# Layer 0 of a two-layer model: the rows for the expert sort are scaled on VectorE instead of GpSimd, and the step order of layer 0 is made anew

## What is computed

```python
xn = _layernorm(x, axis=-1)
x = x + _L0_attn_ref(xn, ...) + _L0_ffn_ref(xn, ...)

def _L0_ffn_ref(x, gate_w, w1, w2, w3):      # 4096 tokens, 8 experts, 2 of them for each token
    scores = jax.nn.softmax(xf @ gate_w, axis=-1)
    top_scores, top_idx = jax.lax.top_k(scores, TOP_K)
    scale = jnp.zeros((T, E)).at[jnp.arange(T)[:, None], top_idx].set(top_scores)
    xs = scale.T[:, :, None] * xf[None, :, :]
    h = jax.nn.silu(jnp.einsum('etd,edh->eth', xs, w1)) * jnp.einsum('etd,edh->eth', xs, w3)
    y = jnp.einsum('eth,ehd->etd', h, w2)
    out = y.sum(axis=0)
```

## Time and profile before

| | us |
|---|---|
| median of 3 runs | 1774.85 (1771.12 to 1778.79) |
| the profiled execution, its own time | 1774.8 |
| its span, first to last instruction | 1773.1 |
| of it layer 0 (last DVE instruction ends at 551.1; layer 1's first at 557.4) | 551 |
| PE busy | 1620.7 |
| DVE busy | 1477.5 |
| POOL busy | 1367.5 |
| ACT busy | 1349.2 |

### The profile page before, as it was taken

How to read it: one execution, slowest core, us unless ns; L and a number is a source line. 1 busy time by engine, 2 the same in 40 slices (tenths; PEclk the granted TensorE clock), 3 DMA queues, 4 the chain that set the end, 5 groups by cost and what they waited for, 6 DMA issues and landing times.

```text
span 1773.1 us, 43498 instructions
## 1 busy us (share of the span) xinstructions
PE 1620.7 (91%) x13450; PEld 987.0 (56%) x13450; DVE 1477.5 (83%) x2750; ACT 1349.2 (76%) x3230; POOL 1367.5 (77%) x1114
## 2 busy tenths in 40 slices
PE   6788999999885888799999999999999999999988
PEld 3455687677563453465465456456556455545545
DVE  5787854356786989899989999999999999998996
ACT  5377877576663868878978978887887897797774
POOL 2059548862671188998999899899899999899995
PEclk9799999999988899999999999999999999999999
DMA  9633446596565743274373464445535446445430
GB/s 326 187 99 121 129 136 205 149 215 193 130 133 161 195 135 115 90 179 109 117 189 101 140 170 123 123 139 126 165 104 146 117 130 177 105 126 161 108 96 25
DMA packets 169963, 252.31 MB, mean 142 GB/s; under 512 B 31144, under 2 KB 114280, under 8 KB 169736
## 3 DMA queue, kind: packets, MB, share of 16 engines
q1 hardware_dynamic: 157448, 232.74, 46.5%
q0 software_dynamic: 12288, 16.79, 4.6%
HBM read 170.44 MB, written 75.86 MB: 139 GB/s over the span
## 4 chain that ended last, share of the span: by engine, by line
PE 37%; DVE 10%; issue 8%; ACT 7%; POOL 5%; DMA 1%; SPq 0%; DVEq 0%; ACTq 0%; POOLq 0%
PE bank L2382 32%; POOL HB L2333 3%; PE bank L2482 3%; DVE bank L2905 3%; DVE HB L2905 2%; ACT bank L2695 2%; POOL HB L2339 2%; DVE SU L2877 2%; ACT PR L2733 1%; DVE HB L2910 1%; ACT PT L2617 1%; PE bank L2510 1%; PE bank L2392 1%; DVE nmax L2936 0%; ACT PR L2726 0%
## 5 line engine op out<-in xcount | busy, mean ns | idle before, releaser
L2333 POOL TENSOR_TENSOR HB<-DD,BC 128x512 f32<-128x512 f32 x512 | 640.9, 1280 | 102.5 <-DMA DD<-SU 48.5
L2695 ACT ACTIVATE bank<-DD,A 128x512 f32<-128x512 f32 x512 | 349.4, 694 | 113.7 <-DVE HB L2910 72.4
L2339 POOL TENSOR_TENSOR HB<-HB,BC 128x512 f32<-128x512 f32 x256 | 324.4, 1284 | 30.7 <-DVE HB L2905 30.1
L2905 DVE TENSOR_TENSOR_SCAN bank<-bank,HB 128x512 f32<-128x512 f32 x256 | 310.8, 1214 | 21.9 <-ACT bank L2695 18.6
L2905 DVE TENSOR_TENSOR_SCAN HB<-bank,HB 128x512 f32<-128x512 f32 x256 | 310.0, 1211 | 10.3 <-ACT bank L2695 7.3
L2910 DVE TENSOR_TENSOR HB<-bank,BC 128x512 f32<-128x512 f32 x256 | 175.4, 685 | 15.9 <-DVE bank L2905 0.9
L2382 PE MATMUL bank<-HB,fold 128*32 128x512 f32 x1024 | 138.3, 612 | 20.5 <-DVE HB L2910 10.8
L743 POOL DMA_INDIRECT X<-expert_out_scratch,slot x64 | 108.0, 1687 | 40.6 <-issue 15.7
L2482 PEld LDWEIGHTS bank<-ident,PR 128*128 128x128 f32 x768 | 86.9, 142 | 82.9 <-issue 45.0
L2482 PE MATMUL bank<-ident,PR 128*128 128x128 f32 x768 | 114.6, 281 | 18.2 <-ACT PR L2733 8.7
L718 POOL TENSOR_SCALAR XSC<-XR,mv,scaled 128x256 f32<-128x256 f32 x64 | 94.2, 1476 | 41.1 <-DVE scaled L1383 36.4
(11 more groups left out here) (287 smaller groups left out, 3568.1 us busy)
## 6 DMA issues: line engine op xcount, KB each, us to landing
DD<-dd_scratch SPq DMA_DIRECT2D x488, 128.0 KB, 3.2
ROW<-row_scratch SPq DMA_DIRECT2D x64, 256.0 KB
BC<-ssm_scratch SPq DMA_DIRECT2D x128, 128.0 KB, 4.0
US<-us_scratch SPq DMA_DIRECT2D x32, 512.0 KB, 4.8
dd_scratch<-SU SPq DMA_DIRECT2D x16, 1024.0 KB, 6.0
us_scratch<-SU SPq DMA_DIRECT2D x15, 1024.0 KB, 6.5
XL<-sorted_scratch SPq DMA_DIRECT2D x78, 128.0 KB
expert_out_scratch<-YS SPq DMA_DIRECT2D x78, 128.0 KB
```

The costliest lines, as they stand in the source:

```text
L2333: done(pool.tensor_tensor(HB[:, c % HR], du, bc, ALU.mult), "dbu")
L2339: done(pool.tensor_tensor(h, h, bc, ALU.mult), "cg")
L2695: done(act.activation(PD[n % 2][:], delta, ACT.Exp, scale=A[:, k:k + 1]), "dA")
L2905: done(dve.tensor_tensor_scan(h if n % 2 else dA, dA, h, 0.0, ALU.mult, ALU.add), "scan")
```

## The change

The function `scaled_rows` and its branch move from POOL's block to DVE's; the instruction, its operands and its three waits stay the same. POOL keeps `sca`. The table `L0_ORDER` is made anew: all 2924 steps stand in it once, as before, with other positions. Against the old table a step of PE stands on average 4 places away within PE's own sequence, one of ACT and one of SP the same. DVE has 870 steps instead of 806, POOL 168 instead of 232. The positions of the steps next to the change are shown; of `tt`, the first tile's transposes, the first entries are 879 and 876 instead of 907 and 895 in the first group, and 1674 and 1679 instead of 1669 and 1672 in the second. Nothing of layer 1 changes.

```diff
-    "agg": [8, 55, 177, 223, 301, 476, 714, 901],
-    "rs1": [11, 57, 179, 225, 306, 649, 843, 905],
-    "xn1": [16, 14, 15, 17, 83, 74, 70, 79, 184, 187, 188, 185, 227, 228, 232, 230, 317, 359, 369, 370, 661, 656,
-        658, 655, 851, 854, 850, 853, 921, 920, 918, 923],
-    "xr": [34, 28, 30, 409, 417, 483, 473, 523, 527, 571, 598, 651, 674, 721, 745, 757, 794, 833, 856, 1096, 1089,
-        1181, 1163, 1240, 1274, 1357, 1345, 1403, 1433, 1481, 1505, 1565],
-    "sx": [357, 396, 406, 364, 415, 471, 463, 429, 499, 518, 522, 506, 550, 558, 586, 541, 641, 615, 663, 606, 713,
-        654, 739, 688, 752, 719, 782, 743, 824, 792, 848, 820, 1071, 1088, 1079, 1061, 1172, 1162, 1138, 1147, 1226,
-        1214, 1261, 1239, 1296, 1343, 1337, 1327, 1353, 1391, 1421, 1417, 1437, 1475, 1489, 1499, 1520, 1557, 1541,
-        1582, 1563, 1618, 1603, 1622],
-    "sca": [373, 441, 424, 386, 455, 490, 481, 448, 509, 526, 533, 514, 596, 580, 630, 569, 681, 626, 696, 617, 725,
-        672, 754, 704, 769, 732, 803, 761, 837, 812, 855, 831, 1132, 1116, 1094, 1108, 1189, 1180, 1220, 1204, 1247,
-        1301, 1286, 1271, 1317, 1361, 1380, 1371, 1400, 1430, 1447, 1460, 1480, 1527, 1504, 1547, 1534, 1587, 1576,
-        1593, 1614, 1638, 1630, 1646],
...
+    "agg": [11, 72, 186, 222, 287, 469, 744, 848],
+    "rs1": [14, 77, 188, 224, 292, 473, 749, 851],
+    "xn1": [20, 18, 19, 17, 81, 83, 87, 84, 192, 196, 195, 193, 230, 229, 231, 228, 351, 300, 355, 312, 529, 523,
+        534, 532, 761, 763, 758, 760, 877, 897, 889, 870],
+    "xr": [26, 2, 8, 393, 443, 453, 479, 522, 524, 557, 580, 645, 651, 704, 732, 770, 759, 818, 842, 1081, 1086,
+        1121, 1181, 1172, 1244, 1246, 1279, 1305, 1332, 1342, 1420, 1395],
+    "sx": [376, 389, 378, 438, 428, 449, 436, 475, 482, 516, 518, 507, 527, 553, 576, 548, 642, 592, 647, 586, 701,
+        660, 726, 725, 765, 694, 757, 753, 814, 747, 838, 824, 1067, 1074, 1078, 1069, 1100, 1115, 1176, 1136, 1154,
+        1167, 1235, 1178, 1212, 1239, 1275, 1242, 1267, 1300, 1320, 1326, 1322, 1335, 1365, 1413, 1392, 1386, 1432,
+        1457, 1448, 1453, 1462, 1510],
+    "sca": [380, 403, 390, 448, 432, 457, 441, 481, 487, 521, 538, 510, 531, 562, 579, 552, 644, 601, 657, 589, 708,
+        668, 737, 728, 773, 699, 762, 784, 817, 755, 841, 830, 1070, 1087, 1102, 1094, 1114, 1126, 1198, 1142, 1160,
+        1174, 1241, 1188, 1220, 1254, 1284, 1259, 1272, 1304, 1324, 1362, 1341, 1351, 1370, 1419, 1398, 1390, 1436,
+        1478, 1451, 1464, 1473, 1514],
...
@@ -706,18 +706,6 @@
                     after(pool, "agg", b, 0)
                     done(pool.tensor_tensor(columns(rstd1[:], b), ve1[:], half[:, 0:NT], ALU.pow), "rs1")
 
-                def scaled_rows(g, i):
-                    x, c = divmod(i, 2)
-                    b, t = batch_tile(g, x)
-                    after(pool, "n", g, RANKS - 1)
-                    k = TT * g + x
-                    pool.wait_ge(over[f"rows_in{k % XRS}"], 16 * (k // XRS + 1))
-                    n = 2 * TT * g + i
-                    if n >= SXS:
-                        pool.wait_ge(moved[f"sort_in{n % SXS}"], 16 * (n // SXS))
-                    done(pool.tensor_scalar(XSC[:, n % SXS], XR[:, k % XRS], columns(mv1[:, :, 0], b)[:, t:t + 1],
-                                            scaled[:, x, c:c + 1], ALU.subtract, ALU.mult), "sx")
-
                 def sort_rows(g, i):
                     x, c = divmod(i, 2)
                     after(pool, "sx", g, i)
@@ -753,8 +741,6 @@
                 for what, b, i in plan:
                     if what == "rs1":
                         input_rstd(b)
-                    elif what == "sx":
-                        scaled_rows(b, i)
                     elif what == "sca":
                         sort_rows(b, i)
                     elif what == "gad":
@@ -1383,6 +1369,18 @@
                         q = dve.tensor_tensor(scaled[:], weight[:], bc(rates, 2), ALU.mult)
                     done(q, "n")
 
+                def scaled_rows(g, i):
+                    x, c = divmod(i, 2)
+                    b, t = batch_tile(g, x)
+                    after(dve, "n", g, RANKS - 1)
+                    k = TT * g + x
+                    dve.wait_ge(over[f"rows_in{k % XRS}"], 16 * (k // XRS + 1))
+                    n = 2 * TT * g + i
+                    if n >= SXS:
+                        dve.wait_ge(moved[f"sort_in{n % SXS}"], 16 * (n // SXS))
+                    done(dve.tensor_scalar(XSC[:, n % SXS], XR[:, k % XRS], columns(mv1[:, :, 0], b)[:, t:t + 1],
+                                           scaled[:, x, c:c + 1], ALU.subtract, ALU.mult), "sx")
+
                 def factors(b):
                     after(dve, "rf", b, 0)
                     after(dve, "sq", b - 1, *range(NT))
@@ -1547,6 +1545,8 @@
                         decayed_values(b, i)
                     elif what == "dc":
                         decays(b, i)
+                    elif what == "sx":
+                        scaled_rows(b, i)
                     elif what == "at":
                         decayed(b, i)
                     elif what == "kv":
```

More of the change, by code:

```diff
@@ L87 @@
 L0_ORDER = {
-    "x_ld": [0, 19, 89, 191, 235, 376, 667, 859],
[4 rows of a table removed]
-    "agg": [8, 55, 177, 223, 301, 476, 714, 901],
[4 rows of a table removed]
-    "xtv": [23, 95, 197, 239, 384, 789, 869, 943],
-    "xta": [24, 97, 198, 242, 387, 783, 885, 940],
[6 rows of a table removed]
-    "vgc": [60, 38, 64, 33, 158, 171, 192, 203, 421, 513, 524, 508, 629, 734, 715, 758, 846, 862, 866, 877, 1650,
[4 rows of a table removed]
-    "smc": [44, 117, 206, 248, 634, 815, 910, 973],
[16 rows of a table removed]
-    "src": [96, 176, 368, 664, 796, 954, 1092, 1748],
-    "qt": [99, 118, 269, 261, 339, 307, 423, 389, 559, 546, 577, 592, 777, 785, 983, 959, 1196, 1120, 1272, 1402,
-        1696, 1667, 2392, 2032, 2448, 2409, 2476, 2502, 2656, 2731, 2720, 2771],
@@ L131 @@
-    "rst": [100, 178, 372, 670, 801, 960, 1254, 1750],
[5 rows of a table removed]
[L137 to L142, removed]
@@ L143 @@
-    "qsc": [123, 128, 214, 266, 351, 326, 501, 457, 549, 547, 660, 722, 930, 903, 1161, 1105, 1292, 1322, 1727, 1692,
[15 rows of a table removed]
-    "rld": [168, 174, 208, 215, 247, 273, 303, 350, 461, 434, 560, 512, 694, 699, 727, 748, 919, 887, 1222, 1145,
[35 rows of a table removed]
-    "ogt": [340, 365, 431, 395, 632, 618, 764, 770, 1003, 1007, 1062, 1076, 1896, 1835, 1968, 1857, 2322, 2362, 2460,
[6 rows of a table removed]
-    "sca": [373, 441, 424, 386, 455, 490, 481, 448, 509, 526, 533, 514, 596, 580, 630, 569, 681, 626, 696, 617, 725,
-        672, 754, 704, 769, 732, 803, 761, 837, 812, 855, 831, 1132, 1116, 1094, 1108, 1189, 1180, 1220, 1204, 1247,
-        1301, 1286, 1271, 1317, 1361, 1380, 1371, 1400, 1430, 1447, 1460, 1480, 1527, 1504, 1547, 1534, 1587, 1576,
-        1593, 1614, 1638, 1630, 1646],
@@ L206 @@
-    "ogc": [391, 410, 437, 425, 636, 627, 873, 776, 1012, 1015, 1068, 1085, 1903, 1839, 1987, 1869, 2327, 2369, 2467,
[55 rows of a table removed]
-    "yst": [955, 967, 1025, 1020, 1027, 1043, 1107, 1101, 1104, 1111, 1187, 1175, 1184, 1202, 1265, 1268, 1257, 1293,
[4 rows of a table removed]
-    "gad": [1716, 1689, 1647, 1656, 1884, 1684, 1959, 1867, 1670, 1664, 1703, 1765, 2041, 1901, 2065, 1983, 1752,
[11 rows of a table removed]
-    "xns": [1874, 1849, 1877, 1890, 1992, 1969, 2128, 2162, 2098, 2104, 2178, 2197, 2334, 2390, 2430, 2235, 2654,
[4 rows of a table removed]
+    "x_ld": [0, 25, 92, 199, 234, 361, 537, 767],
[5 rows of a table added]
@@ new lines @@
+    "agg": [11, 72, 186, 222, 287, 469, 744, 848],
[5 rows of a table added]
+    "xta": [24, 103, 201, 240, 369, 794, 807, 955],
+    "xtv": [27, 99, 202, 241, 368, 800, 844, 958],
[4 rows of a table added]
+    "vgc": [44, 33, 50, 38, 161, 185, 176, 191, 433, 519, 530, 498, 655, 731, 771, 739, 857, 869, 894, 903, 1567,
[6 rows of a table added]
+    "smc": [54, 126, 213, 247, 659, 827, 921, 977],
[10 rows of a table added]
+    "qtc": [95, 109, 270, 275, 350, 314, 412, 395, 600, 567, 638, 635, 890, 854, 994, 966, 1203, 1124, 1312, 1382,
+        1705, 1671, 2418, 2034, 2459, 2402, 2492, 2510, 2628, 2739, 2684, 2778],
@@ new lines @@
+    "src": [98, 194, 367, 646, 820, 942, 1096, 1730],
[3 rows of a table added]
+    "rst": [105, 197, 371, 653, 825, 948, 1256, 1732],
[3 rows of a table added]
+    "ktc": [123, 112, 210, 266, 383, 377, 416, 415, 561, 559, 631, 598, 874, 822, 939, 949, 1223, 1144, 1329, 1430,
[4 rows of a table added]
+    "qst": [122, 121, 211, 259, 332, 320, 517, 461, 566, 547, 670, 709, 918, 885, 1155, 1097, 1245, 1303, 1670, 1678,
+        2066, 2042, 2163, 2225, 2449, 2473, 2543, 2570, 2695, 2734, 2781, 2805],
+    "qsc": [125, 124, 212, 267, 340, 326, 526, 465, 571, 558, 679, 717, 922, 900, 1165, 1109, 1273, 1310, 1680, 1686,
[17 rows of a table added]
@@ new lines @@
```

(10 more changed lines are left out.)

## The result

The changed kernel took 1782.39 us (median of 16 runs, 1772.39 to 1786.05) against 1776.51 us for the kernel before on the same chip (16 runs, 1768.02 to 1782.81): a ratio of 1.0039, 95% interval 1.0024 to 1.0053. A second comparison on another chip gave 1.0027 (1.0007 to 1.0047). It is slower, by 5 to 7 us, where 1 us less was forecast. The time lies in the range given and within 0.5% of the kernel before, but on its wrong side, by more than the comparison is uncertain.

The account below looks back on a forecast made before the run. In group 0's stretch POOL was fullest, but only one wait named it; with the change PE and DVE would both be nearly full. Terms of -2 and +1 us gave -1 from the profiled 1774.8, forecast 1774 us, range 1762 to 1786.

Parts of the forecast that it names:

- The order made anew: Layer 0's new table: PE steps move 4 places on average, about 3 us either sign; 0 in the sum.
- The landing waits: DVE waiting for scatters or row loads to land before a scaling: 0, from above 1 us for each tight place.
- the +1 us of the term: Group 1's stretch, 242 to 330 us: 13.2 us of scaling added to DVE, mostly hidden; from 0 to 3.3, taken +1.
- The price of the scaling: One scaling on DVE costs 414 ns, as line 1501's row; 32 make 13.2 us in each group's stretch.
- The cheap rival: Scaling cheaper on DVE, 284 ns each if streaming halves: -6 us, 1769 us; chance 0.05.
- Group 0's stretch: 104 to 205 us: PE's gap goes, DVE gets the scaling at 93% density; 99.0 us long, -2 us.
- the sum's 92.1: DVE's load in group 0's stretch: 80.1 us, plus 13.2 of scaling, less 1.2 from faster normalisations.
- Line 707: Batch 5's small power, queued on POOL behind scalings and scatters; its wait goes, worth 6.3 us of PE.
- the sum said 1: Whole kernel: -2 us in group 0's stretch and +1 in group 1's, together -1 us.
- POOL's backlog: Rival: POOL held back group 0's stretch; PE gaps of 6.3, 2.1 and 1.7 go, -10.1 us, 1765 us; chance 0.28.
- VectorE as the bound: Rival: DVE bounds group 0's stretch, not packed over 83%; +10, with group 1's 3.3 1788 us; chance 0.23.
- Most likely after 454 us: Where the new order might open or close a gap over 9 us, with no expert tile left to fill PE.

Follow-up runs that it names:

- the move's first measurement: Scaling moved to VectorE with the old order table, against the kernel before, on a chip 1.6% slower: 1.0012 (0.9989 to 1.0036).
- more places: Changed kernel with XN at 7 rows instead of 4 and S2 with a place per batch, against the kernel before: 1774.93 us, 0.9992.
- the move alone: Scaling moved to VectorE with the old order table, against the kernel before: 1769.88 us, 0.9975; on a slower chip 1.0012.
- experiment 6: Against the kernel before: scaling moved to VectorE with the old table, 0.9975; separately, only line 707's power for batch 5 placed right behind its variance, 1.0002.
- The power early: Kernel before with one step moved: line 707's power for batch 5 right behind its variance instead of 172 steps later; 1.0002 (0.9982 to 1.0022).

## Why the prediction was wrong, by its own steps

**The step that failed** is "The order made anew. Each step of PE moves 4 places on average; [...] so about 3 us for a piece of work, either sign: 0 in the sum, 3 us in the range." With the scaling on VectorE in both, the new order costs 12.3 us of medians against the old (1782.2 and 1769.9, on different chips), by the ratios (1.0027 or 1.0039 against 0.9975) 9 to 11 us, and 3 to 5 us if the move's first measurement, 1.0012, is taken. On one chip and with the same early order, the late half of it costs 4 us by itself (1.0027 against 1.0004). All but the lowest of these are over the 3 us allowed. A mean displacement on one engine could not show it. What counted was how many VectorE steps stood in front of a store's landing, how long that store took to land, and what stood behind the wait. The two places can be read in the tables beforehand: three steps instead of six between the store of batch 1's scores and the next score, with `hd` moved from before it to behind it; and for the last batch 7 steps instead of 8, with two stores of rows of x right ahead of the scores' store in SP's queue. Of the 12.3 us, 7 come back when no store is waited for (1782.2 to 1774.9). The other 5 are only a difference of two comparisons whose intervals overlap (0.9992 and 0.9975); whether they are there, and from what cause, stays open. The early order is a candidate: with it and the old late order the ratio is 1.0004 against 0.9975, with intervals that overlap too, and of the 5.7 us by which the traces with more places and with the move alone differ, 3.2 lie before group 1's first result (351.2 and 348.0). Against it speaks that with the new late order the new early one was the faster (1.0027 against 1.0051).

**The landing waits, put at 0 and at 1 us each from above.** With the old table this held: 1.1 us, once. With the new one DVE waited 10.6 us in 9 places in front of the scaling. The dearest are in group 1's stretch. Busy time from 263 to 296 us and from 320 to 345 us, before, then changed:

```profile
263.00:296.00 33.00, 30.93 (x396) 24.08 (x394) 16.10 (x37) 27.13 (x77) 29.25 (x22) 1.00 0.67 209
320.00:345.00 25.00, 22.20 (x210) 13.44 (x209) 9.27 (x16) 11.39 (x39) 20.29 (x15) 0.86 0.60 157
```

```profile
263.00:296.00 33.00, 27.51 (x362) 21.20 (x361) 19.19 (x51) 25.70 (x70) 17.63 (x15) 0.90 0.64 202
320.00:345.00 25.00, 23.43 (x244) 16.12 (x233) 9.62 (x18) 13.71 (x47) 3.21 (x2) 1.00 0.43 127
```

PE was busy 3.4 us less in the first, with a granted clock of 0.90 instead of 1.00, and caught up in the second, where now the kernel before has the gap and the lower clock. Net the first result tile of group 1 came 0.8 us later in these traces, near the +1 us of the term, but by two errors that cancel; on the second chip it came 3.5 us sooner, so nothing bears the term out.

**The price of the scaling** was right: 414 ns forecast, 406 median and 418 mean measured (25.8 us for 64). The cheap rival is out (it asked for 281 or less), and with it the two-port rule of the Trainium skill ("VectorE: DVE Perf Modes", Mode 2x_2P) for this instruction; the trace disagrees, with 406 ns against the 284 that the prediction estimated by it.

**Group 0's stretch.** From the last `n` step to the last scatter 99.0 us were forecast. With the old table it was 98.9 (105.0 to 203.9), though at 86% DVE, not 93: DVE was busy 87.2 us there, not the sum's 92.1, so the length was right by two errors, again. Part of the difference is that VectorE's other instructions, too, were shorter once POOL no longer scaled beside them: the scans took 2281 ns on average instead of 2395, the additions to the state 226 instead of 278; the normalisations' 426 instead of 526 had been counted. With the new table the stretch was 87.8 us (109.7 to 197.5), and 122 of VectorE's attention steps stand between its two ends, where the old table has 131. That the stretch's length passes to the end was not so sure, as experiment 6 shows.

**Line 707.** The gap went, as said, but "worth 6.3 us of PE" is the stretch's worth, not the kernel's: removed by itself it gives nothing measurable (1.0002). The move as a whole, in the old order, gives 0.25% (0.04 to 0.46), 4.4 us, in one comparison and nothing in the other (1.0012), where the sum said 1.

**The rivals.** POOL's backlog at the full 10.1 us is out: without it and in the old order the best that was measured is 4.4 us. The power early (1.0002) tests one of its waits alone, so a smaller worth of the backlog is not excluded. VectorE as the bound is out (PE 92.7 us busy and idle 8.3, its waits for `at` 2.0 in all and none for `kv`, group 0 done 7 us earlier); the measured side was the one that this rival stood for, by a mechanism that none of the rivals held. "Most likely after 454 us" for a gap that the new order opens was half right: one of the two places is at the end, the other at 405 to 426 us, under the tiles.

## What to carry to other kernels

Judge a remade order by its waits, not by how far steps moved: for each wait on a landing in an in-order queue, list what stands between issue and wait, and what stands behind the wait. Change the engine of some work and the order in separate versions, since an order fits the engine it was made for (0.9975 and 1.0205 for the two crossed versions, the latter with the stores freed), and a good half can hide in a bad whole. Where output stores have buffers of one or four places, it is worth enlarging all kinds at once: with one kind enlarged the wait moved to the other.

## What the runs showed of the hardware that was not expected

A scatter whose issue starts while a VectorE scan runs is held until the scan is over. In the changed kernel all five scatters of over 1.6 us between 104 and 205 us lie over one; the first, POOL and then DVE:

```profile
124.94 3.01 POOL L717 DMA_INDIRECT sorted_scratch<-XSC,slot  x1 [0.37 <-DVE XSC L1381]
```

```profile
124.92 2.27 DVE L1414 TENSOR_TENSOR_SCAN dec<-ROW,own_token 128x1024 f32<-128x1024 f32 x1
```

The scan started 0.02 us earlier and ended at 127.19, and the scatter at 127.95, after 3.01 us instead of its 0.96 median; the other four, too, ended some 0.8 us after their scan. A scatter that started 0.3 us ahead of a scan (143.87) took its usual 0.96. So the scatters of group 0 did not stay under the mean of 1.17 us that the prediction named, but had 1.27. The Trainium skill ("SBUF — State Buffer", Who interferes with whom) has the shared port held by an instruction with two SBUF inputs against GpSimd's reads alone, and descriptor writing free of it (the latter marked as inferred there); the trace shows the issue of an indirect DMA held too, whatever it is that it needs.

One chip runs this kernel slower than the others: 1804.66 us against 1773.6 to 1776.5 for the kernel before. The old table with the scaling moved took 1769.88 us elsewhere and 1803.45 there. Most of the difference is in layer 0 (layer 1 starts at 597.4 instead of 553.7 us in the two traces, and takes 1216.6 against 1211.2), and from 104 to 205 us PE is busy about as long at a lower granted clock, 0.86 instead of 0.98, with fewer matmuls recorded (1512 instead of 1675):

```profile
104.00:205.00 101.00, 85.65 (x1512) 52.66 (x1502) 72.28 (x213) 64.20 (x183) 34.17 (x28) 0.86 0.39 112
```

What comes first there, a stall or the clock, no run tells.
